# A routed feed-forward kernel on one core: expert weights 1 to 3 asked for one place sooner, tile 6 turned by VectorE in place of TensorE

## The reference, cut to what matters

```
# x: 4 x 512 tokens of 512; one adapter of four for each batch row
y = x @ W_base.T + scaling * (x @ Wt.T @ A[a].T @ B_w[a].T @ Wp.T)
logits = y @ gate_w.T                       # 16 experts
top 2 of softmax(logits), their weights brought to sum 1
h = silu(y @ w_gate[e].T) * (y @ w_up[e].T) # 352 wide, for each chosen expert e
out = x + sum over the two experts of weight * (h @ w_down[e].T)
```

## Time and profile before

| | |
|---|---|
| median of 3 runs | 341.46 us (339.95 to 343.53) |
| the profiled execution | 341.88 us, of which 340.1 us is the span from first to last instruction |
| TensorE busy | 330.1 us of the span |
| VectorE, ScalarE, GpSimd busy | 233.9, 179.6, 122.6 us |
| moved by DMA | 82.45 MB, mean 242 GB/s |
| granted TensorE clock | 0.998 of 2.4 GHz |

### The profile page before, as it was taken

The page is one execution under the profiler, slowest core; times in us unless marked ns, Lnnn a source line. Parts: engine busy times, 40 slices in busy tenths (PEclk is TensorE's granted clock), DMA queues, the critical chain, the costliest instruction groups (busy, mean ns, idle before and its releaser), DMA issues.

```text
span 340.1 us, 7500 instructions
## 1 busy us (share of the span) xinstructions
PE 330.1 (97%) x1850; PEld 291.4 (86%) x1850; DVE 233.9 (69%) x310; ACT 179.6 (53%) x246; POOL 122.6 (36%) x85
## 2 busy tenths in 40 slices
PE   7999999999999999998999999999999999999993
PEld 5657778889999999987999999999999999999981
DVE  3639799887647577583978849778577579879210
ACT  4369814524465445456548464575545575585321
POOL 0000000013644633637282732846417361434323
PEclk9999999999999999999999999999999999999999
DMA  7975897759698899999999999999999989721144
GB/s 270 415 284 239 308 335 255 263 154 324 236 329 258 221 343 314 233 314 212 304 232 308 296 272 309 170 352 245 293 317 172 342 146 286 152 28 27 17 60 60
DMA packets 47924, 82.45 MB, mean 242 GB/s; under 512 B 5552, under 2 KB 22576, under 8 KB 47792
## 3 DMA queue, kind: packets, MB, share of 16 engines
q1 hardware_dynamic: 38912, 62.96, 56.5%
q0 software_dynamic: 8960, 18.89, 26.7%
HBM read 60.58 MB, written 19.92 MB: 237 GB/s over the span
## 4 chain that ended last, share of the span: by engine, by line
PE 92%; DVE 2%; ACT 2%; DMA 1%; issue 1%; another core or an unknown queue 1%; POOLq 1%; ACTq 0%
PE bank L712 45%; PE bank L741 23%; PE bank L455 4%; PE bank L686 4%; PE bank L492 3%; PE bank L576 3%; PE bank L577 3%; PE bank L578 3%; DMA lead_sb<-lead 1%; PE bank L614 1%; PE bank L629 1%; PE bank L586 1%; ACT w_hi L352 1%; POOLq L96 0%
## 5 line engine op out<-in xcount | busy, mean ns | idle before, releaser
L1285 POOL DMA_INDIRECT out<-ys,sidx x40 | 72.0, 1800 | 123.8 <-DMA out<-ys,sidx 65.7
L1264 POOL DMA_INDIRECT xg<-y_rows,gidx x40 | 50.0, 1251 | 90.7 <-DMA y_rows<-y_st 74.6
L712 PE MATMUL bank<-w_hi,xt_hi 128*128 x320 | 82.1, 333 | 0.3 <-issue 0.3
L354 DVE TENSOR_TENSOR w_lo<-w_raw,w_hi (+2 forms) x32 | 76.1, 2378 | 5.4 <-issue 4.4
L712 PE MATMUL bank<-w_hi,xt_lo 128*128 x320 | 79.1, 324 | 0.0
L712 PE MATMUL bank<-w_lo,xt_hi 128*128 x320 | 79.0, 323 | 0.0
L352 ACT ACTIVATE w_hi<-w_raw (+2 forms) x32 | 64.6, 2020 | 4.4 <-DMA w_raw<-wall 3.7
L876 ACT ACTIVATE sg<-bank 128x352 f32<-128x352 f32 x40 | 18.5, 463 | 82.6 <-PE bank L712 77.7
L712 PEld LDWEIGHTS bank<-w_lo,xt_hi 128*128 128x128 f32 x320 | 56.2, 189 | 0.0
L712 PEld LDWEIGHTS bank<-w_hi,xt_lo 128*128 128x128 f32 x320 | 56.1, 189 | 0.0
L712 PEld LDWEIGHTS bank<-w_hi,xt_hi 128*128 128x128 f32 x320 | 54.6, 189 | 1.6 <-issue 0.9
(11 more groups left out here) (184 smaller groups left out, 363.2 us busy)
## 6 DMA issues: line engine op xcount, KB each, us to landing
w_raw<-wall SPq DMA_DIRECT2D x16, 1408.0 KB
w_raw<-wall SPq DMA_DIRECT2D x16, 768.0 KB
xs<-xg SPq DMA_DIRECT2D x132, 64.0 KB
y_rows<-y_st SPq DMA_DIRECT2D x16, 256.0 KB, 6.7
x_st<-xin SPq DMA_DIRECT2D x6, 512.0 KB, 13.5
lead_sb<-lead SPq DMA_DIRECT2D x4, 512.0 KB, 5.4
head_sb<-head SPq DMA_DIRECT2D x2, 640.0 KB, 8.8
wb_sb<-wb SPq DMA_DIRECT2D x2, 512.0 KB, 11.6
```

What stands on the lines that cost most here:

```text
L354: e.tensor_tensor(lo, raw, hi, ALU.subtract).then_inc(own, 1)
L712: mm = e.matmul(bank[2 + 2 * s + t % 2][:, 0:INTER], a, w[:, bass.ds(at + (k * GU + s * INTER), INTER)], start=k == 0 and i == 0, stop=k = ...
L1264: e.indirect_dma_start(out=xg[t % NXG][:], out_offset=None, in_=y_dram, in_offset=bass.IndirectOffsetOnAxis(ap=gidx[:, t:t + 1], axis=0)). ...
L1285: e.indirect_dma_start(out=out, out_offset=bass.IndirectOffsetOnAxis(ap=sidx[:, t:t + 1], axis=0), in_=ys[t % NYS][:], in_offset=None, bou ...
```

## The change

Four edits. N_PE becomes 6: tile 6 is no longer turned by TensorE but by SyncE's copies and VectorE's transposes. The loads of expert 1 stand behind the store of chunk 11 in place of chunk 15. The wait for `v_w12` moves from SyncE to ScalarE, ahead of the first split into slot 1. SyncE's wait for gather 3 moves from ahead of expert 2's loads to behind them, ahead of expert 3's.

```
-N_PE, NXS = 7, 4
+N_PE, NXS = 6, 4
...
-C_SECOND, N_LATE = CH - 1, 3
+C_SECOND, N_LATE = 11, 3
...
                 if c == C_SECOND:
-                    e.wait_ge(v_w12, 1)
                     for part in PARTS:
                         e.wait_ge(d_w[part], 16)
                         load_part(e, part, table(e, T_REX, 1, 0, NEXP - 1), EW)
...
-            e.wait_ge(d_g[N_LATE], 16)
             e.wait_ge(m_y, CH)
             for part in PARTS:
                 e.wait_ge(d_w[part], 32)
                 load_part(e, part, table(e, T_REX, 2, 0, NEXP - 1), 2 * EW)
+            e.wait_ge(d_g[N_LATE], 16)
             for t in range(N_SOON):
                 later_weights(t)
...
+            e.wait_ge(v_w12, 1)
             split_weights(e, count, 1, ahead, "gu", a_gu)
             x_evac(1)
             silu(0)
```

## The result

| | before | after |
|---|---|---|
| median | 340.70 us (4 runs, 339.77 to 343.53) | 347.91 us (4 runs, 346.66 to 350.68) |
| the profiled execution | 341.88 us, span 340.1 | 349.07 us, span 347.2 |
| TensorE busy | 330.1 us | 334.3 us |
| mean granted clock | 0.998 | 0.981 |

The ratio is 1.0211 (95% interval 1.0153 to 1.0269); 344.4 was forecast, with a range up to 346.2. Both predicted waits are there; both are longer than forecast, and behind each, in the profiled execution, the granted clock falls to half.

The account below looks back on a forecast made before the run. TensorE, working almost without a gap and waiting for no weights, was taken to bound the kernel. The profiled 341.88 us plus 1.95 for h_low(4) plus 1.0 for gather 0 gave 344.8, less 0.42: 344.4 us, range 341.2 to 346.2.

Parts of the forecast that it names:

- Gather 0: Before tile 0's transposes inside chunk 15: held behind expert 1's early load, its rows come 1.0 us late, bounds 0 and 2.6.
- 1.0 us to move and 0 to 1 us to be seen: Gather 0's time from first movement to visible rows, putting tile 0 at 72.7 to 73.7 us.
- the pattern of the same load: Expert 1's load in the kernel before: q0 moved 7.2 us after its issue, so gather 0 would start at 71.7.
- The slower rival: Gather 0 held 8.1 us, as by expert 3's load: TensorE waits 2.4 to 2.6 us in chunk 15, 346.0; chance 0.22.
- The rival in which queues with work take turns: Gather 0 shares the DMA engines with the load and is in time; only late h_low(4) is paid, 343.4; chance 0.22.
- h_low(4): VectorE's remainder of tile 4's hidden rows comes late in the new order: TensorE waits 2.4 us before down(4), 1.95 net.
- the copies are hidden: SyncE's four copies of tile 6, 2.67 us of issue, are done before its rows are wanted after 107.7 us.
- the 98 us: When SyncE would reach the copies of tile 6, gather 6 having landed.
- The clock: Rival: 2.4 us of waiting brings the lower clock, one gate and up costs 3.88 us more, 348.3; chance 0.04.
- ScalarE's stall: At 156.67 us in the kernel before, ScalarE stands 3.09 us, cause unseen; TensorE lost 1.5 us by it.
- "not slower" rival: ScalarE's stall shrinks as loads come sooner: 341.9, 342.9 with gather 0 late, or 339.5 without late h_low(4); chance 0.22.
- Hidden as forecast: Claim that the moved `v_w12` wait, expert 2's earlier loads and stores 12 to 15 behind expert 1's load cost nothing.

Follow-up runs that it names:

- e8: The changed kernel run again without further change, beside e5 on the same chip: 347.74 us, ratio 1.0188 to the kernel before.
- e1: The changed kernel with the loads of expert 1 back behind store 15: 345.87 us, ratio 1.0134 to the kernel before.
- e3: The changed kernel with tile 6 still turned by VectorE, but VectorE's and ScalarE's loops in the old order of steps: 345.96 us, ratio 1.0113.
- e9: The kernel before with one edit alone, expert 2's loads ahead of the wait for gather 3: 342.84 us over 10 runs, ratio 1.0038.
- e5: The changed kernel with unread products of zeros in TensorE's two waits, 20 before tile 0's transposes and 27 before down(4): 346.79 us, ratio 1.0151.
- e7: The changed kernel with only the gu part of expert 1's load behind store 11, the dn part behind store 15: 347.66 us, ratio 1.0206.
- e10: The changed kernel with expert 1's load cut into shorter rows, an eighth of the length in gu, a sixth in dn: 348.98 us, one run.
- e2: The changed kernel with tile 6 turned by TensorE again, the loads still early: 345.11 us, ratio 1.0135 to the kernel before.
- e6: The kernel of e3 with expert 1's loads behind store 14: 347.61 us, ratio 1.0174 to the kernel before.
- e4: The kernel of e3 with expert 1's loads back behind store 15: 342.25 us over 10 runs, ratio 1.0014 to the kernel before.

## Why the prediction was wrong

- **Gather 0, forecast 1.0 us: the term was mis-sized, in the step "1.0 us to move and 0 to 1 us to be seen".** TensorE waited 2.3 to 2.6 us (after, e8). The start was forecast well: by the pattern of the same load at 71.7, measured at 72.2. But from the first packet to the rows in place it took 2.5 us, not 1.5: 1.8 us for the gather's packets and 0.7 us to land. The prediction's own row had it, 79 packets in two microseconds; the 1.0 us came from two gathers that moved together. The slower rival's price, 2.4 to 2.6 us, came true by luck, since it wanted a start 8.1 us behind the load. That pattern was also misread: in the first 3.6 us behind the load of expert 3, 95.4 to 99 us, q0 moved 288 packets, and it stood only after that.
- **The rival in which queues with work take turns** (the Trainium skill, "DMA: Bandwidth & Descriptors", "Queues, rings and completion order") falls as a forecast: gather 0 did not come in time. The rule itself is not refuted. Before 72.2 us no run shows whether q0 had work at the engines, and from then on both queues moved side by side (36 packets of q0 beside 104 of q1 in a microsecond).
- **h_low(4), forecast 2.4 us of waiting and 1.95 net: mechanism right, and the size too where the copies of tile 6 were in time** (2.5 us in e8). The step that failed is "the copies are hidden". No row stood behind the 98 us, and their landing was put at nothing; they came late by 0.57 us in the profiled execution, which waited 3.2 us, and by 2.55 us in e1. e3 removed the wait by the order alone, so the order is shown as its cause. That the two waits could be added was an assumption: e1's second wait is 5.1 us without the early load.
- **The clock, chance 0.04: this step failed.** The prediction read 1.1 us of idling with 1.00 behind it as a sign for 2.4 us. Behind waits of 2.3 to 2.6 us the clock fell in some executions and held in others. Its price, one gate and up more or 3.88 us, was too high for one fall but near what both cost together in the profiled execution, 1.1 and 2.7 us.
- **ScalarE's stall, in the "not slower" rival: it did go in the profiled execution**, 1.9 us back, and hid part of the loss. It is not settled whether chance removed it, and no run shows what it was. But the two edits that cost time are not needed for that: in e9, which has neither, TensorE's wait at that line is 0.3 us, and no other profile has one of 1.5 us.
- **Hidden as forecast:** the wait for `v_w12` and expert 2's loads (e9). Store 15 was hidden only just: it came late with chunk 15, gather 2 went out at 81.89 and not at 77.74, and in e5 TensorE waited 0.8 us for it. No TensorE wait shows weights as its cause in either kernel, so asking sooner had nothing to win.

With the profiled execution's waits its sum would be 341.46 + 3.2 − 0.5 + 2.5 = 346.7, already above the range; beside it stand 346.79 for e5, in which the clock is held, and 347.7 to 347.9 with the clock's share. The stall's 1.9 us are not in this sum and e8's waits are 0.4 us shorter in all, so the agreement is good to a microsecond or two, not closer. For the profiled execution 344.8 was forecast and 349.07 came. By the account above, gather 0 is 1.5 us of the difference, the second wait 0.8 and the half clock 4.4, less 1.9 for the stall and 0.6 of rest.

## What to carry to other kernels

A large load moved ahead on one queue has its price in the small transfers that come behind it: look for what the engines carry, on every queue, in the 8 us after its issue, and for the stores that queue behind it. When a tile's work moves to another engine, write out the whole in-order round on both engines that share it, with the steps that occur only when the data ask for them, and look for the instruction that TensorE waits for behind the new one. Count the landing of a transfer and not only its issue. Count each new TensorE wait of over two microseconds with the lower clock behind it as a case of its own, with a real chance.

## What the hardware showed that was not expected

- A gather issued 3 us behind a load moved nothing for 4.6 us (after), 3.4 us with the gu part alone in front (e7), 3.1 us beside packets an eighth as long (e10) and 1.9 us with no load (before); then it moved beside the rest of the load. Whether its descriptors were posted late or waited in the engines is not shown.
- Six waits of 2.3 to 2.6 us left the clock at 1.00 in four cases (e2, e3, e7's second, e8's first) and brought 0.50 in two (after's first, e8's second), at the same places in the program. The four longer ones, 3.2 to 5.1 us (after, e1, e6, e10), all brought 0.50.
- Cutting the rows of the two loads to an eighth and a sixth made their issue take 6.38 us on SyncE, against 1.32.
- Half a microsecond taken from TensorE, the busiest engine, did not reach the end (e4): the scatters behind it ended last.
